# Edge stage of a graph attention layer on one core: one-hot rows of two turns in one VectorE instruction, both ends in one product, four small chain steps on ScalarE instead of VectorE

## The reference, cut to what matters

```
alpha = einsum(h[src], a_src) + einsum(h[dst], a_dst) + sum(relu(edge_attr @ edge_W.T + b) * h[dst])
alpha = where(alpha >= 0, alpha, 0.2 * alpha)
amax  = segment_max(alpha, dst);  ex = exp(alpha - amax[dst])
attn  = ex / max(segment_sum(ex, dst), 1e-10)
out   = segment_sum(h[src] * attn, dst)
```

## Time and profile before

| what | us |
|---|---|
| median of 3 runs | 3991.97 |
| lowest, highest run | 3991.55, 4013.34 |
| span of the profiled execution | 4846.5 |
| edge stage in that span, first to last `multiply` | 1043 to 3653 |

### The profile page before, as it was taken

One profiled execution on the slowest core, in us unless ns is written; L12 is line 12 of the kernel. 1 busy time (PEld: TensorE's weight loads), 2 busy tenths in 40 slices (PEclk: granted clock), 3 DMA queues, 4 the chain that ended last, 5 costly groups with the idle time before them and its releaser, 6 DMA issues. The chain is left out here.

```text
span 4846.5 us, 80424 instructions
## 1 busy us (share of the span) xinstructions
PE 4087.7 (84%) x22764; PEld 1897.1 (39%) x22765; DVE 2700.2 (56%) x5470; ACT 2291.3 (47%) x6074; POOL 1780.1 (37%) x1859
## 2 busy tenths in 40 slices
PE   5699988957888887788887878878887999999999
PEld 3333322312333333333333333333333666666666
DVE  7566723336666666676666666667666333333333
ACT  4444445524555555555555555555554433333332
POOL 3255555644454445444444444445440000000000
PEclk8799989976888888888888887888887799999999
DMA  7555556655555555555555555555552100000000
GB/s 216 160 165 162 164 177 201 210 156 154 161 168 165 158 165 164 162 168 168 159 162 152 163 157 161 162 159 168 164 162 67 61 8 1 8 8 8 8 8 8
DMA packets 378173, 629.74 MB, mean 130 GB/s; under 512 B 83912, under 2 KB 245063, under 8 KB 377536
## 3 DMA queue, kind: packets, MB, share of 16 engines
q1 hardware_dynamic: 277266, 356.80, 23.4%
q0 software_dynamic: 93408, 257.23, 19.5%
q10 hardware_dynamic: 7104, 11.01, 0.7%
HBM read 520.59 MB, written 104.12 MB: 129 GB/s over the span
## 5 line engine op out<-in xcount | busy, mean ns | idle before, releaser
L1629 POOL DMA_INDIRECT s_rows<-scratch_src_rows,s_idx_w x1312 | 1257.6, 959 | 1367.6 <-PE s_ps_a L1692 563.3
L1837 DVE SCALAR_TENSOR_TENSOR s_enc<-s_enc,s_a_dst,s_ps_d 128x512 f32<-128x512 f32 x904 | 634.9, 741 | 313.3 <-DMA p_feats<-in_edge_f,p_tcol_i 160.8
L1734 ACT ACTIVATE s_enc<-s_ps_f 128x1024 f32<-128x1024 f32 x452 | 459.5, 1017 | 516.6 <-remote 265.5
L1692 PE MATMUL s_ps_a<-s_rows,s_hot_e 128*64 128x264 f32 x3616 | 647.1, 490 | 44.9 <-DVE s_rows L1920 32.4
L2285 DVE SCALAR_TENSOR_TENSOR kx_y_all<-e_ps_o,kx_gate,kx_y_all 128x256 f32 (+1 forms) x392 | 173.5, 480 | 684.2 <-PE e_ps_o L2340 684.2
L1920 DVE TENSOR_TENSOR s_rows<-s_rows,s_ps_x 128x1024 f32<-128x1024 f32 x452 | 545.7, 1207 | 13.6 <-ACT s_a_w L1765 8.7
L1688 PE MATMUL s_ps_a<-ke_sums,k_ident 128*128 x790 | 341.0, 520 | 217.1 <-DVE ke_sums L1913 123.6
L1913 DVE TENSOR_TENSOR ke_sums<-s_ps_a,ke_sums 128x264 f32 x509 | 218.3, 429 | 505.3 <-remote 263.9
L1669 PE MATMUL s_ps_s<-s_enc,s_head_sum 128*32 128x256 f32 x3616 | 353.7, 469 | 152.9 <-DVE s_enc L1837 121.2
L1779 ACT ACTIVATE s_hot_e<-k_iota_row,s_rel_w 128x64 f32<-128x64 f32 x1808 | 480.5, 339 | 0.0
L1787 ACT COPY ke_sums<-s_ps_a 128x264 f32 x395 | 148.6, 376 | 552.5 <-remote 337.8
(11 more groups left out here) (280 smaller groups left out, 5259.0 us busy)
## 6 DMA issues: line engine op xcount, KB each, us to landing
s_table<-scratch_dst_parts SPq DMA_DIRECT2D x904, 96.0 KB
s_rows<-scratch_pre_rows SPq DMA_DIRECT2D x124, 528.0 KB
s_relb<-scratch_rel_rows SPq DMA_DIRECT2D x226, 256.0 KB
scratch_pre_rows<-n_rows SPq DMA_DIRECT2D x62, 528.0 KB
scratch_pre_rows<-m_rows SPq DMA_DIRECT2D x62, 528.0 KB
s_rows<-scratch_src_rows,s_idx_w POOLq DMA_INDIRECT x1312
s_feat<-scratch_step_parts SPq DMA_DIRECT2D x226, 54.0 KB
s_pen_w<-scratch_pen_rows SPq DMA_DIRECT2D x228, 48.1 KB
```

What stands on the lines that cost most here:

```text
L1629: pool.indirect_dma_start(out=rows[:, d % R, m, :], out_offset=None, in_=scr["src_table"], in_offset=bass.IndirectOffsetOnAxis(ap=idx_w[:, ...
L1692: last = PE.matmul(ps_a[t * WN:(t + 1) * WN, sub, 0:SRC_W], hot_e[:, d % 3, 2 * sub + t, :], rows[:, d % R, 2 * sub + t, :], start=(sub == ...
L1734: A.activation(enc[:, d % 2], ps_f[:], ACT.Relu).then_inc(enc_made, 1)
L1837: V.scalar_tensor_tensor(out=enc[:, d % 2, c, :], in0=enc[:, d % 2, c, :], scalar=a_dst[:, c:c + 1], in1=ps_d[:, c, :], op0=ALU.add, op1=A ...
```

## The change

`hot` becomes two buffers of two turns each, and one VectorE instruction fills a pair. It is issued in odd turns: in turn tau for the pair of turns tau + 3 and tau + 4. Two pairs are made before the loop. `relb` is released per pair. Both ends are one `tensor_tensor` with a strided operand. `first` (both halves), the copy into `runs`, `gap` and `fac` are made by ScalarE in the new functions `starts` (turn 1), `keep_run` and `fall` (head of turn 2), and `factors` (turn 3, ahead of `by_edge`). The pair's instruction in turn 1 of a window waits for `starts`, since it overwrites the column that `starts` reads.

```diff
-        hot = s.sb("hot", [P, 2, ED], BF16)
+        hot = s.sb("hot", [P, 2, 2, ED], BF16)
...
                 def load_pair(g):
                     u = g % RP
-                    wait(sp, hot_made, 2 * (g - RP + 1))
+                    wait(sp, hot_made, g - RP + 1)
...
                 def spread_out(d):
-                    u, v = d % RL, d % 2
-                    pe.wait_ge(hot_made, d + 1)
+                    u, v, x = d % RL, d // 2 % 2, d % 2
+                    pe.wait_ge(hot_made, d // 2 + 1)
...
+                def starts(w):
+                    act.wait_ge(hot_made, KW // 2 * w + 1)
+                    wait(act, fac_made, w - 2)
+                    h = hot[:, KW // 2 * w % 2, 0, 0:1]
+                    A.copy(first[:, w % 2, 0:1], h)
+                    A.activation(first[:, w % 2, 1:2], h, ACT.Identity, scale=-1.0, bias=one[:, 0:1]).then_inc(first_made, 1)
+
+                def keep_run(w):
+                    u = w % 2
+                    act.wait_ge(chained, w + 1)
+                    A.copy(runs[:, 1 - u, 0:1], runs[:, u, KS:KS + 1]).then_inc(kept, 1)
+
+                def fall(w):
+                    act.wait_ge(carry_made, w + 1)
+                    wait(act, gain_made, w)
+                    A.activation(gap[:], carry[:, 0:1], ACT.Relu, scale=-1.0, bias=runs[:, w % 2, 2 * KS:2 * KS + 1]).then_inc(gap_made, 1)
+
+                def factors(w):
+                    act.wait_ge(turned_, w + 1)
+                    act.wait_ge(first_made, w + 1)
+                    wait(act, scaled, w - 1)
+                    A.activation(fac[:], ps_g, ACT.Identity, scale=first[:, w % 2, 0:1], bias=first[:, w % 2, 1:2]).then_inc(fac_made, 1)
...
+                    if k == 2 and 0 < w <= NW:
+                        keep_run(w - 1)
+                        fall(w - 1)
...
                     if k == 3 and 0 < w <= NW:
+                        if w > 1:
+                            factors(w - 1)
                         by_edge(w - 1)
+                    if k == 1 and tau < D:
+                        starts(w)
...
-                def spreader(d):
-                    w, k = win(d)
-                    dve.wait_ge(rel_in[d // 2 % RP], 16 * (d // 2 // RP + 1))
-                    wait(dve, spread[1], d - 1)
-                    V.tensor_scalar(hot[:, d % 2, :], relb[:, d // 2 % RP, d % 2, :], p64[:, 0:1], None, ALU.is_equal).then_inc(hot_made, 1)
-                    if k == 0:
-                        dve.wait_ge(hot_made, d + 1)
-                        V.tensor_copy(first[:, w % 2, 0:1], hot[:, d % 2, 0:1]).then_inc(first_hot, 1)
-                        dve.wait_ge(first_hot, w + 1)
-                        V.tensor_scalar(first[:, w % 2, 1:2], first[:, w % 2, 0:1], -1.0, 1.0, ALU.mult, ALU.add).then_inc(first_made, 1)
+                def spreader(g):
+                    dve.wait_ge(rel_in[g % RP], 16 * (g // RP + 1))
+                    wait(dve, spread[1], 2 * (g - 1))
+                    if g >= 2 and (g - 2) % (KW // 2) == 0:
+                        dve.wait_ge(first_made, (g - 2) // (KW // 2) + 1)
+                    V.tensor_scalar(hot[:, g % 2], relb[:, g % RP], p64[:, 0:1], None, ALU.is_equal).then_inc(hot_made, 1)
...
-                    for a, at in ((0, GE - 1), (1, 0)):
-                        last = V.tensor_scalar(ends[:, a, :], turn_of[:, a, :], seg[:, at:at + 1], None, ALU.mult)
-                    last.then_inc(ends_made, 1)
+                    v = seg[:]
+                    at = bass.AP(v.tensor, v.offset + GE - 1, [v.ap[0], [1 - GE, 2], [0, KS]])
+                    V.tensor_tensor(ends[:], turn_of[:], at, ALU.mult).then_inc(ends_made, 1)
...
-                    V.tensor_copy(runs[:, 1 - u, 0:1], runs[:, u, KS:KS + 1]).then_inc(kept, 1)
-
-                def fall(w):
-                    dve.wait_ge(carry_made, w + 1)
-                    V.tensor_scalar(gap[:], carry[:, 0:1], runs[:, w % 2, 2 * KS:2 * KS + 1], 0.0, ALU.subtract, ALU.min).then_inc(gap_made, 1)
...
                 def rescale(w, j):
-                    dve.wait_ge(a_made, w + 1)
-                    V.tensor_scalar(fac[:], ps_g, first[:, w % 2, 0:1], first[:, w % 2, 1:2], ALU.mult, ALU.add).then_inc(fac_made, 1)
...
                 spreader(0)
+                spreader(1)
...
-                    if tau + 1 < D:
-                        spreader(tau + 1)
+                    if tau % 2 == 1 and tau + 3 < D:
+                        spreader((tau + 3) // 2)
```

More of the change, by code:

```diff
@@ L1652, in spread_out @@
                             PE.matmul(ps_d[:, c, sub * GE:(sub + 1) * GE], table[c * 64:(c + 1) * 64, u, sub, C:HALF],
-                                      hot[c * 64:(c + 1) * 64, v, sub * GE:(sub + 1) * GE], start=(sub == 0), stop=False, skip_group_check=True)
+                                      hot[c * 64:(c + 1) * 64, v, x, sub * GE:(sub + 1) * GE], start=(sub == 0), stop=False, skip_group_check=True)
                     for c in range(2):
@@ L1656, in spread_out @@
                             last = PE.matmul(ps_d[:, c, sub * GE:(sub + 1) * GE], table[:, u, sub, c * P:(c + 1) * P],
-                                             hot[:, v, sub * GE:(sub + 1) * GE], start=False, stop=True, skip_group_check=True)
+                                             hot[:, v, x, sub * GE:(sub + 1) * GE], start=False, stop=True, skip_group_check=True)
                         last.then_inc(spread[c], 1)
@@ L1751, in leaked @@
                     A.activation(leak[:], ps_s[:], ACT.Copy, scale=SLOPE).then_inc(leak_made, 1)
+                def starts(w):
[17 more added lines that the diff above has]
+                    A.activation(fac[:], ps_g, ACT.Identity, scale=first[:, w % 2, 0:1], bias=first[:, w % 2, 1:2]).then_inc(fac_made, 1)
                 def exponents(w):
                     act.wait_ge(gap_made, w + 1)
-                    A.activation(gain[:], gap[:], ACT.Exp).then_inc(gain_made, 1)
+                    A.activation(gain[:], gap[:], ACT.Exp, scale=-1.0).then_inc(gain_made, 1)
                     act.wait_ge(shifted, w + 1)
@@ L1869, in carry_on @@
                     dve.wait_ge(chained, w + 1)
+                    wait(dve, gap_made, w)
                     V.tensor_tensor(carry[:], runs[:, u, 0:2 * KS], chain_w[:, u, 1, :], ALU.add).then_inc(carry_made, 1)
-                    V.tensor_copy(runs[:, 1 - u, 0:1], runs[:, u, KS:KS + 1]).then_inc(kept, 1)
-                def fall(w):
-                    dve.wait_ge(carry_made, w + 1)
-                    V.tensor_scalar(gap[:], carry[:, 0:1], runs[:, w % 2, 2 * KS:2 * KS + 1], 0.0, ALU.subtract, ALU.min).then_inc(gap_made, 1)
                 def pick(w):
@@ L1952, in _ @@
                         back(w - 1)
-                    elif chain == 1:
-                        fall(w - 1)
                     elif chain == 2:
```

## The result

| kernel | median, us | lowest to highest | ratio to the kernel before, 95% interval |
|---|---|---|---|
| before | 3994.64 | 3991.55 to 4013.34 | |
| changed | 4419.15 | 4416.53 to 4427.4 | 1.1049 [1.1024, 1.1073] |

The change costs 424.5 us, where 152 were forecast. The direction and both places were right; the size was not.

The account below looks back on a forecast made before the run. VectorE was taken as nearly full, with TensorE nearly equal at full clock. Turn terms summed to +2.7 us a window, times 56 is +152, so 3992 + 152 = 4144 us; range 3960 to 4300.

Parts of the forecast that it names:

- What bounds the kernel: Edge stage: VectorE nearly full in plain runs, 3.84 us a turn, TensorE 3.7; the trace's idle times mostly the profiler's.
- Turn 7's wait, taken at 3.0 us: Pair's instruction in turn 7 waits for `relb`, needed earlier: 3.0 us, bounds 0 and 4.8; turn +2.6 us.
- For three of four pairs that suffices: SyncE issuing `relb` one turn ahead of need: about 5.2 us against 3.7 plus 1.3, called even.
- rival D: TensorE runs dry while VectorE waits and its clock falls: +3.1 us a window, 4318 us; chance 0.13.
- Turn 1's wait, 1.4 us: Pair's instruction in turn 1 waits for ScalarE's `starts`: 1.4 us, bounds 1.2 and 3.1; turn +1.2 us.
- Turn 4 (-0.65): Turn 4 loses one-hot instruction and `fac` on VectorE, 4.35 to 3.65; TensorE's 3.7 takes over: -0.65 us.
- Both ends (0.10): Turn 0: two small products of 0.28 us become one of 0.18, saving 0.10.
- `factors` ahead of `by_edge`, 0.2: Turn 3: `factors` on ScalarE delays `by_edge`, for which VectorE's `weigh` waits: +0.2 us, between 0 and 0.25.
- VectorE's work, 100 us less: Profile after the change: VectorE's busy time should fall by some 100 us.
- rival C: Turns 1 and 7: both waits covered, as other engines set the pace; -1.1 us a window, 3931 us; chance 0.10.
- B's condition: `relb` in time, so turn 7 costs 0, not 2.6: +0.1 us a window, 3998 us; chance 0.12.
- The one-hot pair at 0.39: VectorE's one-hot instruction for 1024 elements takes 0.39 us, between 0.27 and 0.54; 512 elements take 0.27.

Follow-up runs that it names:

- experiment 5: Changed kernel without pairs, one one-hot instruction a turn in its old place: 3932.79 us beside 3995.75 for the kernel before, 0.9852; in the slower condition 1.0002.
- experiment 1: Changed kernel with SyncE issuing `relb` one pair earlier, same buffers and bytes: 4041.4 us beside 3995.75 for the kernel before, 1.012; in the slower condition 1.0082.

## Why the prediction was right or wrong

- *What bounds the kernel*: right in the main. In the quick condition VectorE works 1715 of 1903 us and TensorE 1770, and the turns came out as added up from durations (turn 4 4.29 for 4.35, turns 5 to 7 3.6 for 3.7), except turn 1: 4.9 for 3.9. What fell is the reason that I gave for the long profile: the profiler costs nothing; the machine was in another condition.
- *Turn 7's wait, taken at 3.0 us*: this is the first step that failed. The mechanism was right, its size was not. My own sum from SyncE's rows gave 3.3 to 4.8, and I replaced it by the 2.9 seen in a trace in which turns were 5.7 us long. At 4.2 us a turn VectorE asks earlier and SyncE is as slow. Measured: 4.95 us of idle, turn 7 +4.6 instead of +2.6: 112 us of the 272 missing. The top of the range was worked out with 2 and 4.3 us for the two waits and not with their bounds of 3.1 and 4.8; with these it is 4340, still 79 us short.
- *"For three of four pairs that suffices", "even"*: wrong. The wait in turn 5 was 0.63 us a window and in turn 3 0.36, together 55 us. I had left out L1604: sorted by whether turn 2g - 1 loads ready-made rows, the 13 pairs of turn 5 that do waited 1.8 us each and the other 40 waited 0.2, and in turn 3 it was 1.2 us for 16 pairs and 0 for 37. That is a sorting of one trace; no run took L1604 away.
- *The clock, given to rival D as another case and put at nothing in the sum*: the second step that failed. It fell in every one of the 53 windows (3.4 us of low clock or more), 10.2 us in the mean where the kernel before has 1.7. Turns 0 and 2 grew by 0.56 and 0.89 us where 0.37 and 0.27 were to be saved: 2.1 us a window, 117 us, as much as turn 7's error. For turn 0 the fillers show the clock's part: 0.7 us for the 3.0 us of low clock that they took away. For turn 2 it is argued only: low clock there falls from 3.6 to 1.2 us with `relb` in time and to 0.4 with `first` early, and the turn gets 0.81 and 1.04 shorter, so it takes both waits to make it. D's price of 3.1 us a window was not right either.
- *Turn 1's wait, 1.4 us*: measured 1.84. The wait costs 143 us with `relb`'s waits there and 122 without (4041 to 3919), where 1.2 us a window (67 us) was forecast: beside the kernel without it turn 1 is 1.55 longer, and turns 2 and 3 another 0.3 and 0.4, with 1.2 us of low clock in turn 2. Against the kernel before, turn 1 rose only 0.63, as that turn was 4.9 and not 3.9.
- *Turn 4 (-0.65)*: right, -0.69. *Both ends (0.10)*: 0.27 us to the next instruction before and 0.10 after, 0.17 saved. *`factors` ahead of `by_edge`, 0.2*: turn 3 is 0.54 longer than before even without the waits, and 0.29 without the pairs too (experiment 5); the rest of its 1.28 goes with `relb` (0.36) and `first` (0.38). *VectorE's work, 100 us less*: 71.
- *The gain without waits* (rival C, 3931): 3919 measured. C was right about what remains, but its condition did not hold: both waits are real. B's condition, made true in experiment 1, gave 4041 and not its 3998, since turn 1's wait cost more than 1.2.
- *The one-hot pair at 0.39*: its next instruction starts 0.40 us after it (1806.12 to 1806.52), so the value taken from the rows was right. The estimate of 0.33 came from the formula in the Trainium skill ("VectorE: DVE Perf Modes", section on the TRN2 errata); this trace is above it, as is the page's own measurement.
- *SyncE's queue*: 9.0 to 9.9 us were forecast from the table load to `relb`'s issue, 9.1 measured; 3.5 from issue to reader, 4.0 measured, both in one window.

In sum: of 7.6 us a window, 4.6 is turn 7, 0.6 turn 1, 0.4 turn 5, and 2.7 turns 0, 2 and 3 less 0.7 for turn 4.

## What to carry to other kernels

When an instruction is moved earlier or made to serve two turns, look for what it reads: the moment at which each of its loads is needed moves too, and in a queue that is issued in a fixed order the worst entry decides, not the mean one. Make the sum of a wait at the pace of the runs, not at the pace of the trace, and if span and run times differ by a fifth, find out why before any idle time is read. Here two reorderings that cost nothing, `relb` issued a pair earlier and `first` made in turn 7, turned a loss of 10% into a gain of 2%; the first alone left a loss of 1%.

## What the runs showed of the hardware

- One kernel has two speeds on these machines, 3995 and 4783 to 4853 us, with the same instructions. In the slower one's trace of the kernel before the granted clock of the stage is 0.81 and not 0.96, 199 of SyncE's 1819 MOVE and SEQ_ASSERT instructions took over 0.15 us (none in the quicker one's traces of the kernel before and the changed kernel), and VectorE waits for 264 us in front of the add for what the profile calls "remote". What causes it stays open; no run here was made to tell.
- 12 added matmuls of 512 columns a window did not make the changed kernel longer: the stage's granted clock rose from 0.87 to 0.92, and the time was 4399 us beside 4419.
- The same change costs 10.5% in one condition of the machine and 3.2% in the other, with 445 and 429 us of waiting in front of the pair's instruction.
- The low clock of turn 2 needs both waits: 3.6 us a window with both, 1.2 with the one for `first` alone, 0.4 with the one for `relb` alone.
